# One core, four stages: weight loads on ScalarE's queue, and places of a written-out order moved

## The chip, the cores and the metric

The kernel runs on one core of one Trainium2 chip. Its time is the device time of one execution in microseconds. Before the change the median of 3 runs is 2157.19 us (2152.95 to 2161.05).

## The reference

Four layers follow each other on 2048 tokens of width 1024, in float32. Each is `x = x + layernorm(layer(layernorm(x)))`, except that the last takes x as it is.

- L0 attention: a small state-space network of depth 4 (stage A here).
- L0 feed-forward (stage B): `w2(silu(w1 x) * (w3 x))`, weights that repeat four times along their input, and low-rank parts.
- L1 attention (stage C): `q = x Wq`, `k, v = x Wkv`; 32 heads of queries of width 32 in 8 groups that share k and v; causal softmax; `ctx Wo + bo`.
- L1 feed-forward (stage D): `x W_org`, and a mixture of low-rank parts with softmax coefficients.

The kernel takes the batch of stage C as 2 of 1024 tokens: 16 "heads" of the program (2 batches, 8 groups), each of four query heads.

## The kernel before

**Precision.** Projections run as three passes of a 32-bit format with fewer bits: a value is split into a high part (a ScalarE copy) and a low part (a subtraction on VectorE or GpSimd), and TensorE sums high x high, high x low and low x high. A "part" of a weight matrix is split once, in stage B, and stored to DRAM as `pre_d`. That is done in 36 pieces: ScalarE issues the load (`act_pre_load`, L1263) and makes the high part (`act_pre_hi`, L1275), GpSimd makes the low one (`pool_pre_lo`, L1283), ScalarE issues the store in the next column (`act_pre_store`, L1279). Stage B goes through 16 tiles of 128 tokens with six columns each; every engine has its own written-out order of one column, and a piece is worked on in every second column. TensorE's `pe_fold` (L1108) in column 3 waits for ScalarE's copy `act_xt` of column 2.

**Stage C** is one order of 768 places, S = 48 o + s, for heads o = 0 to 15. At each place TensorE computes a block of scores (`pe_score`, L2086), and one of the blocks of the next heads whose row maxima are needed (`pe_amax`, L2068, 60 places ahead; VectorE takes the maximum, L2381 and L2385). ScalarE takes the exponential (L2253). Every fourth to eighth place TensorE multiplies with V (L2101). GpSimd and VectorE add up P for the softmax's sums; in the heads BY_ROUND (4, 5, 14, 15) TensorE sums half of it. Score banks and maxima banks are rings of three each.

Between them lie the projections ("jobs") of the coming heads. A job is 16 steps of three matmuls in two halves of eight; the list JOBS (L1594) gives the places of the steps and the two places where SyncE's copies of its parts stand. After a half ScalarE copies the high part (`act_job`, c_qh) and VectorE subtracts for the low part (`dve_job`, L2370, c_ql); before the subtraction it waits until the copies of the other half before it have landed. Then SyncE issues twelve DMAs of 64 KB (`sp_place`, L1874 for Q, L1863 for K) that put the parts into Q4 or K4; `pe_amax` of head o reads them first at place 48 o - 60. The weights of a job come by `sp_w` (L1820) from `pre_d` in pieces of 512 KB, and those of the output projection by `sp_wo` (L1828), two DMAs for each of 8 chunks. Both stand on SyncE's queue, at the places `next_at` (one after the last step of a job's third and fourth quarter) and WO_IN.

SyncE's queue is one order too. At each place it has, in this sequence: the steps of `sp_finish` (L1884); the row of maxima of the next head at s = 40 (`sp_mrow`, L1881, read by the first score of the next head); `sp_place`; `sp_w`; `sp_wo`. `sp_finish` turns the sums of half a head into reciprocals for all partitions: step 0 sends the sums to DRAM once ScalarE has copied them (c_cS, s = 6 or 22), step 1 reads them (L1896), VectorE takes the reciprocal, step 2 writes it (L1899), step 3 broadcasts it in four DMAs (L1903), step 4 stores the head's context (L1907). GpSimd then multiplies (`pool_mul`, L2448) in rounds 0 and 4 of the next head; a round is four places. A DMA waits in this queue for its semaphore, and all that is behind it waits too.

RELOAD gives 16 places at which ScalarE's queue brings the split x of batch 1 back, 512 KB each. At the end of stage C the first tiles of the output projection run in TensorE's order (TILES; `pe_early`, L2744); for them ScalarE makes `act_hi`, VectorE `dve_lo` (L2885, both inputs in SBUF). The last maxima (place 707) are turned by TensorE at place 710 (`pe_mrow`, L2074).

## Time and profile before

| | us |
|---|---|
| median of 3 runs | 2157.19 (2152.95 to 2161.05) |
| the profiled execution | 2154.8 |
| its span, at a mean granted clock of 0.973 | 2153.0 |
| TensorE busy | 2002.1 (93%) |
| VectorE, GpSimd, ScalarE busy | 1423.2 (66%), 1064.7 (49%), 933.4 (43%) |

A busy share is the time in which an engine has an instruction running. Times in the rows count from the start of the span. Stage B takes about 390 to 800 us, the 768 places of stage C 958 to 1700 us: about 44 us for an ordinary head.

### The profile page before, as it was taken

Reading aid. Unit: us, or ns where it says so; the run is one execution under the profiler, and the core shown is the slowest. Engines: PE = TensorE matmul, PEld = TensorE weight load, DVE = VectorE, ACT = ScalarE, POOL = GpSimd, SP = SyncE. Lnnn points to the kernel's source line nnn. Section 1 sums busy time; section 2 is a strip of 40 time slices with the busy share of each in tenths; the row PEclk is TensorE's granted clock in tenths of the full one; section 3 lists DMA queues with packets and bytes.
Section 4 is the critical chain, followed back from the end, with each engine's and each line's share of the span. In section 5 each row is a group of like instructions: output and inputs, shape, how many; then the busy total and the mean of one; then the engine's idle time right before and its main releaser. Section 6 shows DMA issues by size and latency. Waiting matters only on the chain. (4 is left out here: it accounts for less than half of the span.)

```text
span 2153.0 us, 30681 instructions
## 1 busy us (share of the span) xinstructions
PE 2002.1 (93%) x10444; PEld 1451.0 (67%) x10444; DVE 1423.2 (66%) x3201; ACT 933.4 (43%) x1938; POOL 1064.7 (49%) x914
## 2 busy tenths in 40 slices
PE   5889886999999999989999899999998999999998
PEld 4644545778788878855666466665654687888887
DVE  7877667777777763177776477677776677654433
ACT  5645685333333323115554455555555433323211
POOL 1444586666666530008886488688884343220000
PEclk9999988999999999989999999999998999999999
DMA  6400376244444338532334643433253385543432
GB/s 188 173 9 1 121 232 230 94 151 167 162 167 167 123 129 305 156 95 57 79 81 111 188 117 80 113 98 97 64 165 117 95 271 183 180 168 132 142 123 97
DMA packets 153435, 292.12 MB, mean 136 GB/s; under 512 B 28750, under 2 KB 69582, under 8 KB 153152
## 3 DMA queue, kind: packets, MB, share of 16 engines
q1 hardware_dynamic: 124224, 241.93, 35.4%
q10 hardware_dynamic: 29056, 48.24, 6.8%
q8 instruction: 83, 1.36, 0.3%
q14 instruction: 72, 0.59, 0.1%
HBM read 163.48 MB, written 94.90 MB: 120 GB/s over the span
## 5 line engine op out<-in xcount | busy, mean ns | idle before, releaser
L2253 ACT ACTIVATE c_P<-PS 128x512 f32<-128x512 f32 (+3 forms) x768 | 349.1, 496 | 342.0 <-PE PS L2086 193.2
L2068 PE MATMUL PS<-c_K,c_Q 96*128 96x512 f32 (+3 forms) x768 | 276.8, 371 | 20.2 <-DVE cst L2385 8.8
L2086 PE MATMUL PS<-c_Q,c_K 97*128 97x512 f32 (+3 forms) x768 | 275.7, 373 | 17.1 <-ACT c_P L2253 9.8
L2498 POOL TENSOR_TENSOR c_S<-c_S,c_P 128x1024 f32<-128x1024 f32 (+3 forms) x94 | 242.0, 2575 | 20.3 <-DVE c_S L2334 12.9
L2086 PEld LDWEIGHTS PS<-c_Q,c_K 97*128 97x128 f32 x768 | 147.4, 193 | 140.0 <-ACT c_P L2253 96.3
L2381 DVE TENSOR_REDUCE cst<-PS 128x1 f32<-128x512 f32 x256 | 175.8, 687 | 77.0 <-PE PS L2068 76.7
L2068 PEld LDWEIGHTS PS<-c_K,c_Q 96*128 96x128 f32 x768 | 149.9, 195 | 77.0 <-DVE cst L2385 28.8
L214 POOL TENSOR_TENSOR maskw<-maskw,mhalf 128x1 f32<-128x1 f32 x64 | 37.7, 590 | 329.9 <-DVE maskw L172 317.6
L1432 DVE SCALAR_TENSOR_TENSOR b_pr<-b_g,b_a 128x460 f32<-128x460 f32 x192 | 180.8, 977 | 1.7
L2385 DVE CUSTOM_DVE_ANT_0 PS<-PS,maskw,cst 128x128 f32<-128x128 f32 (+3 forms) x256 | 142.8, 558 | 53.2 <-PE PS L2068 34.0
L2475 POOL TENSOR_SCALAR_AFFINE_SELECT c_P<-c_P 128x512 f32<-128x512 f32 x128 | 87.4, 683 | 159.8 <-ACT c_P L2253 159.8
L2385 DVE CUSTOM_DVE_ANT_0 PS<-PS,maskw 128x128 f32<-128x128 f32 (+3 forms) x256 | 124.3, 507 | 47.9 <-PE PS L2068 46.3
L1134 PE MATMUL PS<-b_w13h,b_xsh 128*128 128x460 f32 (+1 forms) x384 | 148.0, 385 | 5.9 <-DVE b_xsl L1403 5.9
L2101 PE MATMUL PS<-c_P,c_V 128*32 128x512 f32 (+3 forms) x1536 | 152.3, 502 | 0.4 <-ACT c_P L2253 0.4
L1136 PE MATMUL PS<-b_w13h,b_xsl 128*128 128x460 f32 (+1 forms) x384 | 143.6, 374 | 0.0
L1135 PE MATMUL PS<-b_w13l,b_xsh 128*128 128x460 f32 (+1 forms) x384 | 143.5, 374 | 0.0
L1311 ACT ACTIVATE b_g<-PS 128x460 f32<-128x460 f32 x96 | 53.2, 554 | 202.2 <-PE PS L1136 88.6
L2721 PE MATMUL PS<-c_xth,d_xh 128*128 128x512 f32 x344 | 135.1, 393 | 0.0
L2722 PE MATMUL PS<-c_xtl,d_xh 128*128 128x512 f32 x344 | 134.0, 390 | 0.0
L1530 POOL TENSOR_TENSOR b_gp<-b_g 128x230 f32<-128x230 f32 x96 | 88.9, 926 | 52.6 <-DVE b_g L1417 52.6
L2042 PE MATMUL PS<-c_xth,c_w 128*128 128x512 f32 x272 | 112.3, 413 | 2.0 <-ACT c_V L2199 0.6
L2043 PE MATMUL PS<-c_xtl,c_w 128*128 128x512 f32 x272 | 108.2, 398 | 0.0
(305 smaller groups left out, 4845.5 us busy)
## 6 DMA issues: line engine op xcount, KB each, us to landing
pre_d<-b_pre ACTq DMA_DIRECT2D x36, 512.0 KB, 2.8
c_w<-pre_d SPq DMA_DIRECT2D x34, 512.0 KB, 4.0
a_xin<-in_x SPq DMA_DIRECT2D x32, 512.0 KB, 4.3
d_x<-scr SPq DMA_DIRECT2D x32, 512.0 KB, 4.8
c_Q<-c_qh SPq DMA_DIRECT2D x240, 64.0 KB, 2.0
scr<-a_xin SPq DMA_DIRECT2D x16, 512.0 KB, 5.7
b_xn<-scr SPq DMA_DIRECT2D x16, 512.0 KB, 6.7
b_x<-scr SPq DMA_DIRECT2D x16, 512.0 KB, 5.8
```

Of the source, the lines that this page charges most:

```text
L1134: e.matmul(o, self.xsh[:, par, i, :], wh[:, v, i, :], start=i == 0 and not late, stop=False, skip_group_check=True)
L1135: e.matmul(o, self.xsh[:, par, i, :], wl[:, v, i, :], start=False, stop=False, skip_group_check=True)
L1136: m = e.matmul(o, self.xsl[:, par, i, :], wh[:, v, i, :], start=False, stop=i == 1 and bool(late), skip_group_check=True)
L1432: e.scalar_tensor_tensor(out=self.prod[r][:, 0:n], in0=g, scalar=0.5, in1=self.a2[:, a:a + n], op0=MUL, op1=MUL, accum_out=self.u2[:, r, c ...
L2068: e.matmul(bank[:, 0:hi - lo], self.Q4[0:96, 4 * (o % 3) + g, 128 * t:128 * t + 128], self.K4[0:96, HEADS[o % 8], lo:hi], start=True, stop ...
L2086: e.matmul(self.k.bank(i % 3)[:, 0:hi - lo], self.K4[0:97, HEADS[o % 8], 128 * kt:128 * kt + 128], self.Q4[0:97, 4 * (o % 3) + g, lo:hi], ...
L2101: m = e.matmul(k.bank(5)[32 * g:32 * g + 32, lo - 512 * half:512], self.V[:, kt, o // 8, HEADS[o % 8], :], P[:, g, 0:hi - lo], start=kt == ...
L2253: e.activation(self.P[:, R % 3, g, 0:hi - lo], self.k.bank(i % 3)[:, 0:hi - lo], ACT.Exp, scale=SCALE).then_inc(self.exp_s.s, 1)
L2381: e.tensor_reduce(m, r, AX, ALU.max).then_inc(self.mx_s.s, 1)
L2385: e.tensor_tensor_reduce(out=r, in0=r, in1=self.maskw[:, 512 - n:512], scale=1.0, scalar=m if lo > 0 else -3.0e38, op0=ADD, op1=ALU.max, a ...
L2498: e.tensor_tensor(S[:, gs, 512 - n:512], S[:, gs, 512 - n:512], P[:, gs, 0:n], ADD).then_inc(self.psum_s.s, 1)
L2721: e.matmul(o, h, wh[:, c, cols], start=c == 0, stop=False)
```

## The change

In stage B `act_pre_hi` moves behind the other copies of its column, and `pool_pre_lo` behind `pool_gf` and `pool_x`. In stage C `sp_w` and `sp_wo` become `load_w` and `load_wo`, called in ScalarE's order at the same places after `act_job`, with the same waits. VectorE's part of a job moves one place on. In `q_job` the second half's steps move two places on, and the copies of part 1 one place (from s = 23 to s = 24, where step 0 of `sp_finish` stands ahead of them); K2, K3 and jobs 7 and 11 move by one to five places; RELOAD, WO_IN and TILES have new places; the second half's finish of head 4 comes five places later, with its multiplication in round 7; the early tiles' parts of the output projection move one to three places on. In `StageC.sp` (outside the places) only the two names change.

```
@@ -1342,8 +1342,6 @@
                 if last is not None:
                     self.act_pre_store(e, last)
                 self.act_silu(e, t, c)
-                if p is not None:
-                    self.act_pre_hi(e, p)
                 if c in (0, 2):
                     self.act_ghi(e, t - 1, c // 2)
                 if t == 1 and c < 3:
@@ -1359,6 +1357,8 @@
                         self.act_low(e, t + 1)
                 if t > 1 and c == 4:
                     T.act_x(e, t - 2)
+                if p is not None:
+                    self.act_pre_hi(e, p)
                 if now is not None:
                     self.act_pre_load(e, now)
                 if t == 1 and c == 5:
@@ -1549,12 +1549,12 @@
                     T.pool_y(e, t - 1)
                 if t + 1 < NT and c == 3:
                     self.pool_xsum(e, t + 1)
+                self.pool_gf(e, t, c)
                 p = self.pre_at(t, c, 1)
+                if t > 1 and c == 3:
+                    T.pool_x(e, t - 2)
                 if p is not None:
                     self.pool_pre_lo(e, p)
-                self.pool_gf(e, t, c)
-                if t > 1 and c == 3:
-                    T.pool_x(e, t - 2)
                 if t == 1 and c < 3:
                     self.w2lo(e, 2 * c)
         T.pool_x(e, 14)
@@ -1585,7 +1585,7 @@
 def q_job(o):
-    return o, q_slots(48 * o - 112, 2, 48 * o - 94, 2), (48 * o - 95, 48 * o - 73)
+    return o, q_slots(48 * o - 112, 2, 48 * o - 92, 2), (48 * o - 95, 48 * o - 72)
@@ -1593,19 +1593,19 @@
 JOBS = [("K0", None, None), ("K1", None, None), (0, None, None), (1, None, None), (2, None, None)]
 JOBS += [q_job(3), q_job(4), q_job(5), (6, q_slots(172, 2, 190, 2), (194, 206)),
-         ("K2", q_slots(208, 1, 219, 1), (217, 228)), (7, q_slots(231, 1, 243, 1), (242, 260)), q_job(8), q_job(9), q_job(10),
-         ("K3", q_slots(405, 1, 416, 1), (414, 425)), (11, q_slots(428, 1, 438, 2), (437, 454)), q_job(12), q_job(13),
+         ("K2", q_slots(208, 1, 220, 1), (218, 233)), (7, q_slots(235, 1, 247, 1), (245, 262)), q_job(8), q_job(9), q_job(10),
+         ("K3", q_slots(407, 1, 418, 1), (416, 427)), (11, q_slots(430, 1, 441, 2), (439, 457)), q_job(12), q_job(13),
          q_job(14), q_job(15)]
 JOB = {job[0]: n for n, job in enumerate(JOBS)}
-RELOAD = [239 + 2 * n for n in range(4)] + [255 + 2 * n for n in range(4)] + [263 + 3 * n for n in range(8)]
-WO_IN = {644 + 6 * c: c for c in range(8)}
-TILES = {711 + 4 * n: (0, n) for n in range(8)} | {745 + 4 * n: (1, n) for n in range(5)}
+RELOAD = [244 + 2 * n for n in range(4)] + [256 + 2 * n for n in range(4)] + [264 + 2 * n for n in range(8)]
+WO_IN = {644 + 8 * c: c for c in range(8)}
+TILES = {714 + 4 * n: (0, n) for n in range(8)} | {747 + 4 * n: (1, n) for n in range(5)}
 LAST = [(14, r) for r in range(7, 12)] + [(15, r) for r in range(6, 12)]
@@ -1912,7 +1912,7 @@
     def finish_at(self, S, step):
-        late = 5 if S >= 720 or 432 <= S < 480 else 0
+        late = 5 if S >= 720 or 240 <= S < 288 or 432 <= S < 480 else 0
         first, second = ((S - f[step] - d) // 48 if (S - f[step] - d) % 48 == at else -1
                          for f, at, d in zip(self.FINISH, (16, 0), (0, late)))
         return 2 * first if first >= 0 else 2 * second - 1 if second > 0 else None
@@ -1973,10 +1973,6 @@
                     self.sp_mrow(e, o + 1)
                 if S in self.place_at:
                     self.sp_place(e, *self.place_at[S])
-                if S in self.next_at:
-                    self.sp_w(e, *self.next_at[S])
-                if S in WO_IN:
-                    self.sp_wo(e, WO_IN[S])
                 if S in (692, 724, 746):
                     self.then.sp_first(e, S)
         self.sp_finish(e, 30, 4)
@@ -2298,17 +2294,21 @@
                     self.act_evac(e, 2 * o, 0)
                 if S in self.evac_at:
                     self.act_job(e, *self.evac_at[S])
+                if S in self.next_at:
+                    self.load_w(e, *self.next_at[S])
+                if S in WO_IN:
+                    self.load_wo(e, WO_IN[S])
                 if S in RELOAD:
                     self.act_reload(e, RELOAD.index(S))
                 if s == 39 and o < 15:
                     self.act_mrow(e, o + 1)
                 if S in (699, 701):
                     self.then.act_hi(e, 0, (S - 699) // 2)
-                if S in (727, 743):
-                    self.then.act_hi(e, 1, int(S > 727))
+                if S in (728, 744):
+                    self.then.act_hi(e, 1, int(S > 728))
                 if S == 758:
                     self.then.act_y(e, 0)
-                if S == 760:
+                if S == 762:
                     self.then.act_hi(e, 2, 0)
         self.act_evac(e, 31, 0)
@@ -2414,8 +2414,8 @@
                 A = S + 48 + LEAD
                 if A < 768:
                     self.dve_amax(e, A // 48, A % 48)
-                if S in self.evac_at:
-                    self.dve_job(e, *self.evac_at[S])
+                if S - 1 in self.evac_at:
+                    self.dve_job(e, *self.evac_at[S - 1])
                 if s in (27, 28) and o not in BY_ROUND:
                     self.dve_pair(e, o, s - 25)
                 if s in (35, 36) and (o, BOTH) not in LAST and o < 15:
@@ -2426,16 +2426,16 @@
                 for n in {708: [0], 712: [1], 716: [2], 720: [3], 724: [4], 747: [5], 751: [6], 757: [7], 761: [8]}.get(S, ()):
                     for g in range(4):
                         self.dve_last(e, n, g)
-                if S == 704:
+                if S == 707:
                     for half in range(2):
                         self.then.dve_lo(e, 0, half)
-                if S in (729, 744):
-                    self.then.dve_lo(e, 1, int(S > 729))
-                if S == 746:
+                if S in (730, 745):
+                    self.then.dve_lo(e, 1, int(S > 730))
+                if S == 748:
                     self.then.dve_y(e, 0)
                 if S == 755:
                     self.then.T[0].dve_y_nm(e, 0)
-                if S == 762:
+                if S == 764:
                     self.then.dve_lo(e, 2, 0)
         for n in (9, 10):
             for g in range(4):
@@ -2474,7 +2474,7 @@
                 if lo == 128 * kt:
                     e.affine_select(out=P[:, :, 0:128], in_=P[:, :, 0:128], compare_op=ALU.is_ge, fill=0.0, base=0,
                                     pattern=[[0, 4], [1, 128]], channel_multiplier=-1).then_inc(self.diag_s.s, 1)
-                if o > 0 and r in ((0, 7) if o in (9, 15) else (0, 4)):
+                if o > 0 and r in ((0, 7) if o in (5, 9, 15) else (0, 4)):
                     self.pool_mul(e, 2 * o - (2 if r == 0 else 1))
                 if (o, r) == (15, 7):
                     self.then.T[0].pool_y(e, 0)
```

## Rows read from the trace of the kernel before

**Rows 1.** Who waited for whom, TensorE, 950 to 1700 us: total us, times, longest us.

```profile
PE PS L2086 <- ACT c_P L2253: 9.8, 25, 3.8
PE PS L2086 <- DMA c_Q<-c_mT: 7.2, 3, 5.1
...
PE PS L2074 <- DVE cst L2385: 5.4, 3, 3.2
...
PE PS L2744 <- ACT c_mT L2212: 0.8, 1, 0.8
...
PE PS L2042 <- DVE c_ql L2370: 0.5, 1, 0.5
```

**Rows 2.** Windows: length; busy us by engine; granted clock; DMA share; GB/s.

```profile
1192.00:1199.00 7.00, 6.52 (x17) 5.36 (x18) 2.92 (x9) 2.39 (x4) 1.88 (x2) 0.52 0.69 195
...
1229.80:1233.20 3.40, 3.40 (x13) 2.23 (x15) 1.24 (x3) 1.96 (x5) 3.40 (x2) 0.50 0.96 250
1612.10:1618.90 6.80, 6.66 (x36) 4.55 (x36) 3.46 (x13) 3.26 (x6) 6.63 (x7) 0.50 0.68 248
1649.60:1656.40 6.80, 6.04 (x20) 3.59 (x20) 6.67 (x12) 1.57 (x6) 0.64 (x1) 0.50 0.24 82
```

**Rows 3.** Time line of SyncE's queue, 1176 to 1189 us: start, us, instruction.

```profile
1176.52 0.32 SPq L1899 DMA_DIRECT2D rec_d<-cst  x1
...
1183.05 1.22 SPq L1863 DMA_DIRECT2D c_K<-c_qh  x2
...
1186.04 1.98 SPq L1903 DMA_DIRECT2D c_cS<-rec_d  x4
1188.12 0.53 SPq L1881 DMA_DIRECT2D c_Q<-c_mT  x1
```

**Rows 4.** Time line of GpSimd in head 5; in brackets idle us before.

```profile
1225.13 1.27 POOL L2448 TENSOR_TENSOR c_cH<-c_cH,c_cS 128x512 f32<-128x512 f32 x1 [11.27 <-DMA c_cS<-rec_d]
```

**Rows 5.** Time line of TensorE at place 288; landing of L1881's 16 DMAs.

```profile
1249.16 0.50 PE L2086 MATMUL PS<-c_Q,c_K 97*128 97x512 f32 x1 [0.69 <-DMA c_Q<-c_mT]
...
DMA to landing us min/median/max: 2.1/2.2/4.3
```

**Rows 6.** Time lines of SyncE's queue and TensorE, place 672.

```profile
1607.90 0.53 SPq L1881 DMA_DIRECT2D c_Q<-c_mT  x1
...
1612.24 0.80 PE L2086 MATMUL PS<-c_Q,c_K 97*128 97x512 f32 x1 [1.37 <-DMA c_Q<-c_mT]
```

**Rows 7.** Time lines of VectorE and GpSimd, places 706 to 711.

```profile
1642.26 4.74 DVE L2885 TENSOR_TENSOR d_xl<-d_in,d_xh 128x512 fp32r<-128x512 f32 x2
...
1642.88 2.38 POOL L2467 TENSOR_TENSOR c_S<-c_S,c_P 128x1024 f32<-128x1024 f32 x1
```

**Rows 8.** Who waited for whom: TensorE in stage B; ScalarE's SiLU, whole span.

```profile
PE PS L1108 <- ACT b_xT L1254: 3.5, 4, 1.2
...
ACT b_g L1311 <- POOL b_pre L1285: 18.5, 16, 1.4
```

**Rows 9.** Time lines of TensorE and ScalarE, head 12; landing of L1874's DMAs.

```profile
1543.11 0.44 PE L2068 MATMUL PS<-c_K,c_Q 96*128 96x384 f32 x1 [0.32 <-DVE cst L2381]
...
1546.15 0.58 ACT L2261 COPY c_cS<-PS 128x512 f32<-128x512 f32 x1
...
1556.65 0.23 PE L2068 MATMUL PS<-c_K,c_Q 96*128 96x128 f32 x1
...
DMA to landing us min/median/max: 1.9/2.0/6.9
```

**Rows 10.** Time lines of VectorE and TensorE, head 9.

```profile
1412.39 0.69 DVE L2370 TENSOR_TENSOR c_ql<-PS,c_qh 128x512 fp32r<-128x512 f32 x1 [0.76 <-ACT c_qh L2206]
...
1423.52 0.30 PE L2068 MATMUL PS<-c_K,c_Q 96*128 96x128 f32 x1
```

**Rows 11.** Lines L2227 (ScalarE's queue) and L1820 (landing): ns min/median/max.

```profile
L2227 ACTq DMA_DIRECT2D c_xth<-x_d x8: 366/366/388, 1187.2 to 1242.3; - x8
...
DMA to landing us min/median/max: 3.3/4.0/8.5
```

More of the change, by code:

```diff
@@ L1344, in act @@
                 self.act_silu(e, t, c)
-                if p is not None:
-                    self.act_pre_hi(e, p)
                 if c in (0, 2):
@@ L1361, in act @@
                     T.act_x(e, t - 2)
+                if p is not None:
+                    self.act_pre_hi(e, p)
                 if now is not None:
@@ L1551, in pool @@
                     self.pool_xsum(e, t + 1)
+                self.pool_gf(e, t, c)
                 p = self.pre_at(t, c, 1)
+                if t > 1 and c == 3:
+                    T.pool_x(e, t - 2)
                 if p is not None:
                     self.pool_pre_lo(e, p)
-                self.pool_gf(e, t, c)
-                if t > 1 and c == 3:
-                    T.pool_x(e, t - 2)
                 if t == 1 and c < 3:
@@ L1586, in q_job @@
 def q_job(o):
[L1588 removed]
+    return o, q_slots(48 * o - 112, 2, 48 * o - 92, 2), (48 * o - 95, 48 * o - 72)
 JOBS = [("K0", None, None), ("K1", None, None), (0, None, None), (1, None, None), (2, None, None)]
 JOBS += [q_job(3), q_job(4), q_job(5), (6, q_slots(172, 2, 190, 2), (194, 206)),
[L1596 to L1597 removed]
+         ("K2", q_slots(208, 1, 220, 1), (218, 233)), (7, q_slots(235, 1, 247, 1), (245, 262)), q_job(8), q_job(9), q_job(10),
+         ("K3", q_slots(407, 1, 418, 1), (416, 427)), (11, q_slots(430, 1, 441, 2), (439, 457)), q_job(12), q_job(13),
          q_job(14), q_job(15)]
 JOB = {job[0]: n for n, job in enumerate(JOBS)}
[L1601 to L1608 removed]
+RELOAD = [244 + 2 * n for n in range(4)] + [256 + 2 * n for n in range(4)] + [264 + 2 * n for n in range(8)]
+WO_IN = {644 + 8 * c: c for c in range(8)}
+TILES = {714 + 4 * n: (0, n) for n in range(8)} | {747 + 4 * n: (1, n) for n in range(5)}
 LAST = [(14, r) for r in range(7, 12)] + [(15, r) for r in range(6, 12)]
@@ L1801, in sp_wv, with load_w @@
                     ).then_inc(self.wld[n].s, 16)
-    def sp_w(self, e, m, half):
+    def load_w(self, e, m, half):
         if m >= len(JOBS) - 1:
@@ L1913, in finish_at @@
     def finish_at(self, S, step):
-        late = 5 if S >= 720 or 432 <= S < 480 else 0
+        late = 5 if S >= 720 or 240 <= S < 288 or 432 <= S < 480 else 0
         first, second = ((S - f[step] - d) // 48 if (S - f[step] - d) % 48 == at else -1
@@ L1934, in sp_first @@
         elif i == 2:
-            self.sp_w(e, 0, 0)
-            self.sp_w(e, 0, 1)
+            self.load_w(e, 0, 0)
+            self.load_w(e, 0, 1)
             self.sp_x(e, 4)
@@ L1945, in sp @@
             if u == 11:
-                self.sp_w(e, 1, 0)
-                self.sp_w(e, 1, 1)
-        self.sp_w(e, 2, 0)
+                self.load_w(e, 1, 0)
+                self.load_w(e, 1, 1)
+        self.load_w(e, 2, 0)
         for n in (0, 1):
@@ L1951, in sp @@
                 self.sp_place(e, n, part)
-        self.sp_w(e, 2, 1)
+        self.load_w(e, 2, 1)
         self.sp_place(e, 2, 0)
-        self.sp_w(e, 3, 0)
-        self.sp_w(e, 3, 1)
+        self.load_w(e, 3, 0)
+        self.load_w(e, 3, 1)
         self.sp_place(e, 2, 1)
-        self.sp_w(e, 4, 0)
+        self.load_w(e, 4, 0)
         self.sp_place(e, 3, 0)
-        self.sp_w(e, 4, 1)
-        self.sp_w(e, 5, 0)
+        self.load_w(e, 4, 1)
+        self.load_w(e, 5, 0)
         self.sp_place(e, 3, 1)
@@ L2300, in act @@
                     self.act_job(e, *self.evac_at[S])
+                if S in self.next_at:
+                    self.load_w(e, *self.next_at[S])
+                if S in WO_IN:
+                    self.load_wo(e, WO_IN[S])
                 if S in RELOAD:
@@ L2306, in act @@
                     self.then.act_hi(e, 0, (S - 699) // 2)
-                if S in (727, 743):
-                    self.then.act_hi(e, 1, int(S > 727))
+                if S in (728, 744):
+                    self.then.act_hi(e, 1, int(S > 728))
                 if S == 758:
                     self.then.act_y(e, 0)
-                if S == 760:
+                if S == 762:
                     self.then.act_hi(e, 2, 0)
@@ L2428, in dve @@
                         self.dve_last(e, n, g)
-                if S == 704:
+                if S == 707:
                     for half in range(2):
                         self.then.dve_lo(e, 0, half)
-                if S in (729, 744):
-                    self.then.dve_lo(e, 1, int(S > 729))
-                if S == 746:
+                if S in (730, 745):
+                    self.then.dve_lo(e, 1, int(S > 730))
+                if S == 748:
                     self.then.dve_y(e, 0)
@@ L2437, in dve @@
                     self.then.T[0].dve_y_nm(e, 0)
-                if S == 762:
+                if S == 764:
                     self.then.dve_lo(e, 2, 0)
@@ L2476, in pool @@
                                     pattern=[[0, 4], [1, 128]], channel_multiplier=-1).then_inc(self.diag_s.s, 1)
-                if o > 0 and r in ((0, 7) if o in (9, 15) else (0, 4)):
+                if o > 0 and r in ((0, 7) if o in (5, 9, 15) else (0, 4)):
                     self.pool_mul(e, 2 * o - (2 if r == 0 else 1))
```

16 lines of the change are left out of this document (3 added, 13 removed).

## The prediction

> **What bounds the kernel now.** I read the views in this order: the page, for the busy shares; who waited for whom on TensorE, for the attention stage; the windows, for the clock after each long wait; then the time line of each engine that ends such a wait. TensorE is busy 93% of the span, so only its waits, and the clock that they cost, can be won. In the attention stage (958 to 1700 us) the waits fall into two kinds [rows 1]: many of 0.2 to 0.7 us in the ordinary heads, and a few long ones: 5.1 us for c_mT's copy (7.2 in 3), up to 3.8 us for an exponential, up to 3.2 us for the maxima that the transpose at L2074 reads. After the long ones the windows show the granted clock at 0.50 to 0.52 (1.2 GHz) for 3.4 to 6.8 us, with TensorE busy in them [rows 2]: it then does half of what it does at 2.4 GHz, so such a window costs half its length: 3.4 + 1.7 + 3.4 + 3.4 us.
>
> **What each long wait is.** (1) Before place 240, 5.12 us. SyncE's queue is the late one: rec_d at 1176.52, twelve copies of K2's second part up to 1186.0, four broadcasts, and only at 1188.12 the row of maxima [rows 3]. (2) In head 5 an exponential waits 3.8 us [rows 1], because GpSimd stood 11.27 us, until 1225.13, for the broadcast that its multiplication takes, with all sums of P behind it [rows 4]. (3) Before place 288, 0.69 us, again that row; it landed 4.3 us after its issue at worst, where 2.2 is the median [rows 5]. (4) Before place 672, 1.37 us: issued at 1607.90, landed about 1612.2 [rows 6]. (5) At place 710, 3.24 us, and 0.76 behind it for the first early tile: VectorE's two special subtractions took 4.74 us where one is 0.7, beside GpSimd's sum at 1642.88 [rows 7].
>
> **The change part by part** (gains are minus).
>
> *Low parts and copies in the feed-forward stage.* The high copy goes behind the copies of the next tile, so L1108 no longer waits: 3.5 us in 4 waits [rows 8]. Against it: GpSimd's low part now stands behind two sums (1.03 and 0.65 us), and ScalarE's store, which precedes the next SiLU, waits for it; it already did so 16 times, 18.5 us [rows 8]. In column 0 the SiLU of column 1 comes about 1.1 us later, and the product behind it has some 0.9 us before TensorE asks: 0 to 0.4 us in each of 12 tiles. Between -3.5 and +1.3 us; I take -3.0, since late loads (the usual case) already keep GpSimd at that time.
>
> *Place 240.* K2's second part goes from place 228 to 233, behind the row of maxima (232). From rec_d at about 1177 the broadcasts follow when it has landed (some 2 us) and take 2 us; the row is issued at about 1181 instead of 1188.1 and lands by 1183.5, against TensorE at 1187.4: the 5.1 us and the half clock behind them go: **-8.5**. What is late next is the second part: its twelve copies end at 1189.5 and land 2 us later, as VectorE's part of job 7 (now place 244, about 1191.8) asks for them: none to 0.5 us. K2's second half one place later takes the wait for c_ql: **-0.5** [rows 1].
>
> *Head 5.* The multiplication goes from round 4 to 7, sums of head 4 five places on. The 3.8 + 1.7 + 0.7 us go if nothing else is late. But SyncE, by my count: part 0 of job 7 until about 1200, write and read of the sums 1202.6, reciprocal 1207, broadcasts 1210 to 1212, part 1 of job 7 until 1218 to 1219.6, with TensorE at place 276 (the first use of it) at about 1222. The reloads of x1, 16 of them and now two places apart, run beside it; a copy then landed after up to 6.9 us where 2.0 is the median [rows 9]. So a wait of 0 to 3 us at 276, and as much again for the row before 288. I take 3.0 of the 6.2 back: **-3.2**, between -6.2 and +2.
>
> *Ordinary heads.* Second halves start at place 4 instead of 2 and end at 18 instead of 16. The VectorE part of a job moves one place on. What goes is part of the two waits around places 20 to 22 (the longer 0.32 [rows 9]), where TensorE had no projection beside the scores. The copies of part 1 now stand at place 24, behind the send of the sums, which waits for c_cS of place 22. In head 12 that copy began at 1546.15; its end 0.6, the send 0.6, twelve copies at 0.63 each (two took 1.22 and a gap [rows 3]), and 1.4 from the end of the last issue to landing (the median of 2.0 from its start, less 0.6) make 1556.2, and the maxima that read it start at 1556.65 [rows 9]: a margin of 0.4 us, which the faster head uses up. Net **-3.0** for ten such heads, between -5 and +5.
>
> *Head 9.* Job 11's second half ends at place 455 instead of 452; c_ql came at 1412.39, the maxima that read its copies start at 1423.52 [rows 10]. Three to four places later is 1416; with 7.5 and 1.4 us that is 1425.3: about 2 us of waiting, and half a chance of 1.7 us of clock: **+2.9**, between 0 and +5.
>
> *Loads on ScalarE's queue.* 27 pieces and 16 of Wo. No wait of theirs is open when ScalarE gets there: TensorE has done the step one place earlier. An issue there is 0.37 us and lay beside a running exponential [rows 11]. Cost 0; if it did stand in the way, 43 x 0.37 = 16 us, less what the ring of three banks absorbs; below nothing if SyncE's freed 0.4 us each lets copies out. I take 0, the nearest row.
>
> *Place 672.* Without Wo on SyncE the row goes out 0.5 us earlier, but the broadcasts before it wait for the landing of rec_d. Wo's 1 MB pieces every 8 places instead of 6 still run beside it. The copies of job 15 land later too (Wo's first pieces now run beside them), which costs at place 660 what 672 no longer does. Of 1.37 + 3.4 I take **-2.3**, between 0 and -4.8.
> The Trainium skill, "DMA: Bandwidth & Descriptors", section "Issuing engines are not separate DMA queues", says that DMAs of all issuing engines share the same engines and that a second issuer only saves issue time; the same page's "Queues, rings and completion order" says that a DMA engine alternates between queues. By the first the row still takes 4.3 us, by the second it would not stand behind Wo. The trace bears out the first: before place 288 the row was just as slow with the bulk on ScalarE's queue [rows 5].
>
> *Place 710.* The last maximum is of place 707, and the two subtractions go behind it (704 to 707): the transpose waits for nothing of theirs. Early tile (0, 0) at 714 no longer meets c_mT's copy (0.76). All 4.0 + 3.4 us go, less 0.5 for VectorE's sums, now 0.5 late for the exponential of 712: **-6.9**, between -7.4 and -3.
> The Trainium skill, "SBUF — State Buffer", section "Who interferes with whom", has a VectorE instruction with two SBUF inputs wait for the whole of a GpSimd one that reads SBUF; the 4.74 us agree. By it the subtraction, reached at about 1644.5, would still be held until 1645.3, off the path.
>
> Sum: -3.0 - 8.5 - 0.5 - 3.2 - 3.0 + 2.9 - 2.3 - 6.9 = -24.5 us. The profiled execution took 2154.8 us (span 2153.0), so 2130.3 for it; the median of the runs is 2.4 us above it, so **2132.7**, say 2133.
>
> **Rivals.** (A) *The moved places become waits.* The copies of head 5 and head 9 and the row before 672 stay as late as now; nothing is won in ordinary heads or in the feed-forward stage: -8.5 - 0.5 - 6.9 + 4 = -12, 2145. For it: landings of 4 to 7 us while loads run [rows 5, 9]; against it: SyncE is free of loads. (B) *Small copies are freed from the bulk.* The row lands in 2.2 us everywhere: 672 wins 4.8 and head 5 some 5: 2129. Against it: place 288. (C) *Slower: part 1 behind the sums.* The margin of 0.4 us is negative in the 11 heads whose part goes at place 24 or later. With loads beside it a copy lands 4 instead of 2 us after issue: 1.6 to 2 us of waiting per head, and from about 1.4 us, as at 672, the clock halves after it. 11 x (1.4 + 1.7) = 34 us against 27.4 won elsewhere: +7, 2164; it decides once copies land some 1.8 us later than the median. Against it: the loads of those heads are issued at places 11 and 19, and such a load landed 4.0 us after its issue [rows 11], before the copies end. (D) *The row of maxima doesn't hang on SyncE's order* but on VectorE's reciprocal, and the new order only shifts the wait: within 3 us of 2157.
>
> **How the numbers follow.** Forecast 0.55, A 0.22, B 0.08, C 0.08, D 0.07. What a measurement can tell from no change is about 0.5%, 10.8 us, that is 2146.4 and 2168. Faster: forecast, B and three quarters of A: 0.80; same: the rest of A and D, 0.12; slower: 0.08. The lowest sum of the bounds that I believe at once is -36 (2121); above, A reaches to 2147. Range 2120 to 2147.
>
> **What would show it.** At place 240 and at 710 no wait over 0.5 us and no half clock behind them; L1108 without waits; the row of maxima of head 5 issued before K2's second part; no GpSimd wait of 11 us in head 5. A wait of L2068 for c_Q's copies at places 276 and 468 of 1 to 3 us shows the two costs; such a wait in every ordinary head shows C. The forecast is wrong if the long waits come back at the next place, or if ScalarE's exponentials start late behind load issues.

## The result and the profile after

The changed kernel takes **2179.66 us** (median of 4 runs, 2174.78 to 2183.68) against 2155.7 us for the kernel before in the same session: ratio 1.0107 [1.0076, 1.0139]. It is 1% slower where 1% faster was forecast. The profiled execution took 2174.78 us, its span is 2173.1 us, the mean granted clock 0.977. Stage C's lines stand 4 lower than before (L2086 is now L2082, L2068 L2064, L2129 L2125, L2253 L2249); stage B's are the same.

By stages and heads of the two traces (from the first score of a head to that of the next; the last column is the changed kernel with stage B's two moves undone, e1 below):

| us | before | after | forecast | found | e1 |
|---|---|---|---|---|---|
| stage B, first to last up-projection | 451.9 | 481.7 | -3.0 | **+29.8** | 451.7 |
| heads 4 and 5 (places 192 to 287) | 116.6 | 110.6 | -12.2 | -6.0 | 109.7 |
| ten ordinary heads | 448.4 | 448.4 | -3.0 | 0.0 | 447.7 |
| head 9 | 45.8 | 53.1 | +2.9 | +7.3 | 51.9 |
| heads 13, 14, 15 | 132.5 | 122.4 | -9.2 | -10.0 | 121.8 |
| everything else | 957.8 | 956.8 | 0 | -1.0 | 959.5 |

The profiled execution is the fastest of its four, so the traces differ by 20.1 us where the medians differ by 24.

First who waited for whom on TensorE in the whole span (engine, line, what it waited for: total us, times, longest us). Before, the first of these lines was 7.9 us in 3 waits, 6.6 of them in one at the start of the stage; from 390 us on the gated value, b_g, was late once, by 0.2 us.

```profile
PE PS L1156 <- DVE b_g L1417: 29.3, 13, 4.9
...
PE PS L1134 <- DVE b_g L1417: 6.5, 11, 0.8
```

Nearly all of it lies in stage B. There TensorE stands idle 40 us instead of 15: 25 of the 30 us; the other 5 are longer busy time, for which no cause is shown. VectorE's product waits for ScalarE's SiLU, and the same view of ScalarE, from 390 to 870 us, says why that is late; its first line stood at 18.5 us in 16 waits [rows 8]:

```profile
ACT b_g L1311 <- POOL b_pre L1285: 67.4, 24, 3.3
...
ACT b_y L234 <- DMA pre_d<-b_pre: 44.9, 11, 4.3
```

The second existed before as well, once:

```profile
ACT b_y L234 <- DMA pre_d<-b_pre: 2.0, 1, 2.0
```

The time line of ScalarE in columns 4 and 5 of one tile (start, us, instruction, in brackets idle us before), kernel before:

```profile
425.59 0.61 ACT L1277 CAST b_pre<-b_raw 128x512 fp32r<-128x512 f32 x1
...
427.60 0.34 ACTq L1281 DMA_DIRECT2D pre_d<-b_pre  x1
...
432.44 0.38 ACTq L1271 DMA_DIRECT2D b_raw<-in_wq  x1
433.45 1.21 ACT L234 ACTIVATE b_y<-PS,maskw 128x1024 f32<-128x1024 f32 x1 [0.76 <-DVE maskw L180]
435.04 0.55 ACT L1311 ACTIVATE b_g<-PS 128x460 f32<-128x460 f32 x1 [0.38 <-PE PS L1156]
```

and the same column after:

```profile
426.65 1.25 ACT L239 ACTIVATE b_y<-b_x,maskw 128x1024 f32<-128x1024 f32 x1 [0.56 <-DVE maskw L207]
427.80 0.60 ACT L1277 CAST b_pre<-b_raw 128x512 fp32r<-128x512 f32 x1
430.35 0.33 ACTq L1281 DMA_DIRECT2D pre_d<-b_pre  x1
...
436.77 0.38 ACTq L1271 DMA_DIRECT2D b_raw<-in_wq  x1
437.20 1.21 ACT L234 ACTIVATE b_y<-PS,maskw 128x1024 f32<-128x1024 f32 x1 [4.27 <-DMA pre_d<-b_pre]
438.31 0.55 ACT L1311 ACTIVATE b_g<-PS 128x460 f32<-128x460 f32 x1
```

The high copy starts 2.2 us later, behind the long L239; GpSimd's low part, the next row, starts at 429.03, where it was at 426.28; so the store goes out 2.75 us later.

```profile
429.03 1.29 POOL L1285 TENSOR_TENSOR b_pre<-b_raw,b_pre 128x512 fp32r<-128x512 f32 x1
```

**And the next load, in ScalarE's own order, waits until that store has landed** (`act_pre_load` waits on `pre_out`, though what it overwrites, `raw`, is last read by the low part). Now the store lands at 436.75, 6.4 us after its issue, and ScalarE stands in front of the load, with L234 and the next SiLU behind it; the row of L234 shows 4.27 us. One late copy has become a late SiLU, product and rank matmul (L1156).

The trace before had this wait already, at its limit. The same store (427.60) took

```profile
DMA to landing us min/median/max: 4.8/4.8/4.8
```

so it landed at 432.42, and the load went out 0.02 us later: ScalarE already stood at it, for 0.3 us at most, and this lay within the 0.76 us for which L234 had to wait for VectorE anyway. Of the 35 loads of that kernel that wait for a store, 24 went out 0.02 us behind its landing; in the changed kernel all 35 do. ScalarE's view of waits does not show this, since it lists waits of computing instructions and not of DMA issues: one has to set the landing of each store beside the issue of the load behind it. Of the 4.3 us by which this load is later than before, 2.75 are the later store and 1.6 its slower landing; two transfers of 512 KB that SyncE had issued at 428.3 and 428.8 ran beside it until 434.2 and 435.5.

In the attention stage, TensorE from 978 to 1725 us, against [rows 1]:

```profile
PE PS L2064 <- DVE cst L2385: 11.4, 21, 2.9
PE PS L2125 <- POOL c_S L2498: 6.3, 11, 0.6
PE PS L2082 <- ACT c_P L2249: 4.0, 14, 0.6
...
PE PS L2064 <- DMA c_Q<-c_qh: 2.9, 1, 2.9
...
PE PS L2125 <- DVE cst L2385: 2.0, 1, 2.0
...
PE PS L2038 <- DVE c_ql L2370: 1.0, 1, 1.0
PE PS L2082 <- DMA c_Q<-c_mT: 0.9, 1, 0.9
```

The three waits for c_mT's copy (7.2 us) are one of 0.9, the exponential's 9.8 are 4.0, and the transpose's 3.2 and the early tile's 0.8 are gone: those moves did what they were to do. Other waits have come. The long ones with their places, 262 and 277 in head 5, 454 in head 9, and 661 in head 13. (From here on a wait has the number of the next score behind it. The maximum or sum that waits stands one place earlier in the order: 277, 469 and 661 are the 276, 468 and 660 of the prediction.)

```profile
1241.22 0.44 PE L2064 MATMUL PS<-c_K,c_Q 96*128 96x384 f32 x1 [2.90 <-DVE cst L2385]
...
1259.12 0.44 PE L2064 MATMUL PS<-c_K,c_Q 96*128 96x128 f32 x1 [2.58 <-issue]
...
1439.16 0.64 PE L2125 MATMUL PS<-c_S,cst 128*32 128x512 f32 x4 [2.03 <-DVE cst L2385]
...
1633.59 0.30 PE L2064 MATMUL PS<-c_K,c_Q 96*128 96x128 f32 x1 [2.92 <-DMA c_Q<-c_qh]
```

Beside each, from 0.1 us before its end to 0.9 us behind it, begins a stretch at half the clock, as those of [rows 2] (length; busy us by engine; granted clock; DMA share; GB/s):

```profile
1241.90:1248.70 6.80, 6.80 (x33) 3.73 (x24) 2.97 (x10) 3.44 (x7) 3.41 (x2) 0.50 0.60 172
1259.00:1262.40 3.40, 3.27 (x14) 1.90 (x14) 0.90 (x3) 0.49 (x1) 1.72 (x1) 0.50 0.83 297
1439.90:1443.30 3.40, 3.40 (x11) 2.39 (x8) 2.00 (x5) 2.06 (x4) 2.38 (x1) 0.50 0.25 80
1634.50:1637.90 3.40, 3.40 (x17) 0.84 (x10) 0.87 (x4) 0.98 (x2) 2.90 (x1) 0.50 0.40 119
```

The first wait is VectorE's: it stands in front of a reciprocal, with the maxima behind it.

```profile
1240.49 0.25 DVE L2390 RECIPROCAL cst<-cst 128x16 f32<-128x16 f32 x1 [2.97 <-DMA cst<-sum_d]
```

SyncE's queue shows the sums' way to that reciprocal, and the copies of job 7's second part:

```profile
1229.82 0.53 SPq L1891 DMA_DIRECT2D sum_d<-c_cS  x1
1235.36 0.34 SPq L1896 DMA_DIRECT2D cst<-sum_d  x1
1240.78 0.33 SPq L1899 DMA_DIRECT2D rec_d<-cst  x1
1243.19 1.71 SPq L1903 DMA_DIRECT2D c_cS<-rec_d  x4
1245.01 0.52 SPq L1874 DMA_DIRECT2D c_Q<-c_qh  x1
...
1251.92 0.60 SPq L1874 DMA_DIRECT2D c_Q<-c_qh  x1
1252.56 0.53 SPq L1891 DMA_DIRECT2D sum_d<-c_cS  x1
```

The write of the sums and their read (a few KB each) take 5.5 and 5.1 us beside the reloads, with the DMA engines 99% busy. In the kernel before the same write held SyncE from 1203.5 to 1209.7, and away from the reloads 1.7 us (1257.5 to 1259.2); the copies end at 1252.5, TensorE asks for them at 1256.5.

### The profile page after: what moved, and what is told of

The parts are those of the page before. It is cut to its first block, busy times and chain, and to the rows that moved or that the text cites. A ratio compares the mean times of both kernels' runs of the same rounds, so it can differ in the third digit from the quotient of the medians.

```text
span 2173.1 us, 30680 instructions
## 1 busy us (share of the span) xinstructions
PE 1998.2 (92%) x10444; PEld 1449.0 (67%) x10444; DVE 1396.3 (64%) x3201; ACT 932.3 (43%) x1938; POOL 1071.2 (49%) x914
## 3 DMA queue, kind: packets, MB, share of 16 engines
q8 instruction: 83, 1.36, 0.3%
## 4 chain that ended last, share of the span: by engine, by line
PE 52%; POOL 12%; DVE 11%; DMA 7%; issue 7%; ACT 4%; SPq 4%; ACTq 2%; POOLq 0%; DVEq 0%
PE PS L2721 5%; PE PS L2722 5%; PE PS L2725 5%; PE PS L2082 4%; POOL c_S L2498 4%; PE PS L2064 4%; PE PS L2097 3%; DMA pre_d<-b_pre 3%; SPq L1874 3%; POOL b_pre L1285 2%; PE PS L2038 2%; PE PS L663 2%; PE PS L2039 2%; PE PS L2040 2%; DVE PS L2385 2%
## 5 line engine op out<-in xcount | busy, mean ns | idle before, releaser
L2249 ACT ACTIVATE c_P<-PS 128x512 f32<-128x512 f32 (+3 forms) x768 | 348.7, 496 | 328.4 <-PE PS L2082 188.0
L2064 PE MATMUL PS<-c_K,c_Q 96*128 96x512 f32 (+3 forms) x768 | 275.5, 369 | 30.2 <-DVE cst L2385 13.4
L2082 PE MATMUL PS<-c_Q,c_K 97*128 97x512 f32 (+3 forms) x768 | 272.5, 369 | 4.8 <-ACT c_P L2249 4.0
L2498 POOL TENSOR_TENSOR c_S<-c_S,c_P 128x1024 f32<-128x1024 f32 (+3 forms) x94 | 241.9, 2574 | 22.2 <-DVE c_S L2334 13.8
L2082 PEld LDWEIGHTS PS<-c_Q,c_K 97*128 97x128 f32 x768 | 146.9, 192 | 125.5 <-ACT c_P L2249 90.4
L2064 PEld LDWEIGHTS PS<-c_K,c_Q 96*128 96x128 f32 x768 | 148.9, 194 | 85.1 <-DVE cst L2385 38.0
L1432 DVE SCALAR_TENSOR_TENSOR b_pr<-b_g,b_a 128x460 f32<-128x460 f32 x192 | 161.3, 876 | 1.7
L1417 DVE TENSOR_TENSOR b_g<-b_g,PS 128x460 f32<-128x460 f32 x96 | 60.3, 629 | 127.7 <-ACT b_g L1311 127.6
```

The costliest lines, as they stand in the source:

```text
L1432: e.scalar_tensor_tensor(out=self.prod[r][:, 0:n], in0=g, scalar=0.5, in1=self.a2[:, a:a + n], op0=MUL, op1=MUL, accum_out=self.u2[:, r, c ...
L2064: e.matmul(bank[:, 0:hi - lo], self.Q4[0:96, 4 * (o % 3) + g, 128 * t:128 * t + 128], self.K4[0:96, HEADS[o % 8], lo:hi], start=True, stop ...
L2082: e.matmul(self.k.bank(i % 3)[:, 0:hi - lo], self.K4[0:97, HEADS[o % 8], 128 * kt:128 * kt + 128], self.Q4[0:97, 4 * (o % 3) + g, lo:hi], ...
L2249: e.activation(self.P[:, R % 3, g, 0:hi - lo], self.k.bank(i % 3)[:, 0:hi - lo], ACT.Exp, scale=SCALE).then_inc(self.exp_s.s, 1)
L2498: e.tensor_tensor(S[:, gs, 512 - n:512], S[:, gs, 512 - n:512], P[:, gs, 0:n], ADD).then_inc(self.psum_s.s, 1)
```

## The experiments

Each kernel was timed in turns with the kernel before on the same chip; the ratio is to that. Where two kernels' ratios lie within 0.5% of each other, I call it no difference in the time, though a trace can still place it; each trace is of one execution, and stage B or the 768 places differ by up to 5 us between kernels that are equal there.

**e1: stage B as before.** The changed kernel with both moves of stage B undone:

```
                 self.act_silu(e, t, c)
+                if p is not None:
+                    self.act_pre_hi(e, p)
...
                     T.act_x(e, t - 2)
-                if p is not None:
-                    self.act_pre_hi(e, p)
...
+                p = self.pre_at(t, c, 1)
+                if p is not None:
+                    self.pool_pre_lo(e, p)
                 self.pool_gf(e, t, c)
-                p = self.pre_at(t, c, 1)
                 if t > 1 and c == 3:
                     T.pool_x(e, t - 2)
-                if p is not None:
-                    self.pool_pre_lo(e, p)
```

> The changed kernel with both moves in stage B (the high copy late in its column, the low part behind GpSimd's sums) undone. Theory 1 (the loss is in stage B alone: 451.9 -> 481.7 us between the first and last up-projection, while stage C won 8.7): stage B takes 452 again, 1.008 less stage C's gain: 2150 us, ratio to before 0.996. Rival (stage C's gain in the trace of the changed kernel exists only because stage B's waits left its start calmer): 2156 or more, ratio 1.00.

2144.75 us, ratio 0.9947 [0.9933, 0.9961]. Stage B is 451.7 us again, and the 768 places take 731.0 us against 743.2. So the slower time is stage B's alone; the rest of the change is worth about 11 us in the time (8.7 to 12.2 by the 768 places of the two traces), half of the forecast 21.5.

**e2 and e3: the two moves of stage B, one at a time**, each put into the kernel before. e2, and below it e3:

```
                 self.act_silu(e, t, c)
-                if p is not None:
-                    self.act_pre_hi(e, p)
...
                     T.act_x(e, t - 2)
+                if p is not None:
+                    self.act_pre_hi(e, p)
```

```
-                p = self.pre_at(t, c, 1)
-                if p is not None:
-                    self.pool_pre_lo(e, p)
                 self.pool_gf(e, t, c)
+                p = self.pre_at(t, c, 1)
                 if t > 1 and c == 3:
                     T.pool_x(e, t - 2)
+                if p is not None:
+                    self.pool_pre_lo(e, p)
```

> The kernel before with only ScalarE's high copy moved late in its column. Theory L (a loop: in column 4 the copy waits behind the 1.25 us normalisation of an older tile, so the store goes out 2.2 us later, and in column 5 ScalarE stands at the next load until that store has landed, with the normalisation and the next SiLU behind it; slack today 1 us): about +1.2 us and more in each of 12 tiles, less 3.5 us for L1108: 2166 to 2172. Rival G (the cost is GpSimd's order, the low part behind two sums, met by the SiLU of columns 1 and 3): nothing lost here, 3.5 us won, 2152.

> The kernel before with only GpSimd's low part moved behind its sums. Theory L: the store of column 4 goes out 1.8 us later and lands 0.8 us after the slack ends: +10 us, 2166. Rival G: nearly the whole loss of stage B, 2180 to 2185.

e2: 2172.69 us, 1.0076 [1.0063, 1.0089], stage B 465.7. e3: 2197.31 us, 1.0189 [1.0176, 1.0202], stage B 488.7. Each makes the store late by itself and has the wait for its landing, the same view of ScalarE in e2:

```profile
ACT b_y L234 <- DMA pre_d<-b_pre: 36.0, 11, 3.6
```

and in e3:

```profile
ACT b_y L234 <- DMA pre_d<-b_pre: 41.6, 11, 3.9
```

The moves do not add (13.8 and 36.8 us alone, 29.8 together), and e3 took far more than the 2166 us that I expected, more even than its rival's 2180 to 2185. In e3 TensorE waits at L1108 as well, 14.7 us in 11 waits, longest 1.5: the load comes late, ScalarE's high copy still stands ahead of the copy that L1108 reads, and waits for it. Only the first move takes this path away, as the forecast had it for the kernel before; these waits are 14.7 of the 31 us by which e3 lies above its expectation, and the rest stays open.

**e5: the load no longer behind the store.** The whole changed kernel; the load waits for the low part, the last reader of its buffer `raw`, and the high copy, the first writer of `pre`, waits for the store:

```
 def act_pre_load(self, e, p):
     if p > 0:
-        e.wait_ge(*self.pre_out(p))
+        e.wait_ge(*self.pre_lo(p))
...
 def act_pre_hi(self, e, p):
     e.wait_ge(*self.pre_in(p + 1))
+    if p > 0:
+        e.wait_ge(*self.pre_out(p))
```

> The whole changed kernel, with one wait of stage B at another place: the load of the next piece waits for the low part of the piece before (which ends the reading of b_raw), and no longer for its store to land; the high copy waits for that instead (it overwrites b_pre). Theory L (ScalarE stands at the load until the store has landed, 4.3 us in column 5 in the trace of the changed kernel, and the next load lands late for the copies of column 0 and 2): most of the 30 us come back, stage B 452 to 460 us instead of 481.7, 2150 to 2160. Rival G (only GpSimd's order counts: the low part behind its sums, met by the SiLU of columns 1 and 3): at most 5 us, 2175 or more.

2145.53 us, 0.9954 [0.9937, 0.9971]; stage B 451.2 instead of 481.7 us, with both moves still in. ScalarE in the same column (lines behind the edit two higher):

```profile
428.03 0.60 ACT L1279 CAST b_pre<-b_raw 128x512 fp32r<-128x512 f32 x1
430.58 0.33 ACTq L1283 DMA_DIRECT2D pre_d<-b_pre  x1
...
432.59 0.38 ACTq L1271 DMA_DIRECT2D b_raw<-in_wq  x1
433.89 1.21 ACT L234 ACTIVATE b_y<-PS,maskw 128x1024 f32<-128x1024 f32 x1 [0.77 <-DVE maskw L180]
435.49 0.55 ACT L1313 ACTIVATE b_g<-PS 128x460 f32<-128x460 f32 x1 [0.38 <-PE PS L1156]
```

Copy and store are as late as in the changed kernel (430.58), the load goes out at 432.59 and nothing stands. The wait of ScalarE for GpSimd's low part has even grown in e5, and costs nothing:

```profile
ACT b_g L1313 <- POOL b_pre L1287: 80.4, 24, 4.4
```

So the load's wait for the landing accounts for the 30 us, and the wait that I had priced was nearly harmless. The rival, GpSimd's order alone, had at most 5 of them come back.

**e11: the same edit in the kernel before** (the diff of e5).

> The kernel before with only the wait for the store moved from the load to the high copy. Theory L (that wait is the loop of stage B): the load lands 3 us earlier, so the high copy no longer holds up the copies behind it; L1108's 3.5 us go: stage B 448.5, 2153. Rival (the load then lands earlier but the high copy waits for the store instead): no difference, 2156.

2155.26 us, 0.9988 [0.9978, 0.9998]; in the trace stage B is 447.9 us (451.9) and L1108's waits are gone, which is what the moves of stage B were forecast to give; the whole time does not tell it from no change. Beside it e5, with the same free load and both moves, is 3.3 us longer in this stage (451.2), within the spread of such traces: with the load free the moves show no gain over the old order.

**e7: the loads back on SyncE's queue**, the rest as e1 (below: in `sp`; the same four lines go from `act`).

```
+                if S in self.next_at:
+                    self.sp_w(e, *self.next_at[S])
+                if S in WO_IN:
+                    self.sp_wo(e, WO_IN[S])
```

> The first kernel again (stage B as before, stage C as changed), but all weight loads back on SyncE's queue at the same places. Theory 4 (the move of the loads to ScalarE's queue is worth nothing by itself; the places are): 2143 to 2147 as the first kernel. Rival (it is what makes the new places possible: 12 copies, four broadcasts and the row of maxima are each held up by a load's wait for TensorE): 5 us and more above it, 2150 or more, with the row of head 5 or 6 late again.

2144.58 us, 0.9944 [0.9928, 0.9959]: equal to e1 (0.9947). Which queue issues the loads makes no difference in the time. It only shifts a wait; TensorE around places 661 and 672 in e7

```profile
1598.45 0.30 PE L2068 MATMUL PS<-c_K,c_Q 96*128 96x128 f32 x1 [0.57 <-DMA c_Q<-c_qh]
...
1610.73 0.80 PE L2086 MATMUL PS<-c_Q,c_K 97*128 97x512 f32 x1 [1.95 <-DMA c_Q<-c_mT]
```

and in e1:

```profile
1602.74 0.30 PE L2064 MATMUL PS<-c_K,c_Q 96*128 96x128 f32 x1 [3.20 <-DMA c_Q<-c_qh]
```

In e1 TensorE has no wait at place 672, having lost more time at 661 already.

**e4: head 9 as before**, the rest as e1:

```
-("K3", q_slots(407, 1, 418, 1), (416, 427)), (11, q_slots(430, 1, 441, 2), (439, 457))
+("K3", q_slots(405, 1, 416, 1), (414, 425)), (11, q_slots(428, 1, 438, 2), (437, 454))
```

> Stage B as before, stage C as changed, but K3 and job 11 at their places of before. Theory 2 (head 9 costs 7.3 us since job 11's part 1 is copied three places later and is read by the maxima at place 468, with 3.4 us of half clock behind an earlier wait of 2.0 us): 7 us less than the first kernel of this call, 2143. Rival (the wait only moves on to the next row of maxima, since GpSimd's sums or SyncE's finish steps are late by themselves): within 2 us of it.

2146.25 us, 0.9948 [0.9935, 0.9961]: no gain over e1. Head 9 is 46.5 us instead of 51.9, but head 8 is 56.1 instead of 51.5, with waits for c_ql of 1.06 and 1.26 us and a half-clock window of 3.4. Head 9's price is not in the moves of K3 and job 11 taken alone.

**e6: K2's second part alone behind the row of maxima**, in the kernel before:

```
-("K2", q_slots(208, 1, 219, 1), (217, 228))
+("K2", q_slots(208, 1, 219, 1), (217, 233))
```

> The kernel before with one number changed: the copies of K2's second part at place 233 instead of 228 in SyncE's order, behind the row of maxima. Theory 3 (that order alone made the 5.1 us at place 240 and the half clock behind it): -8.5 us, 2147.5, and job 7's low part waits less than 1 us for the copies. Rival (the load pieces on SyncE's queue, still there, hold the row up all the same): 2156.

2158.61 us, 1.0012 [1.0000, 1.0023]. The wait before place 240 goes and comes back before place 244, longer than it was:

```profile
1197.27 0.80 PE L2068 MATMUL PS<-c_K,c_Q 96*128 96x512 f32 x1 [6.07 <-DVE cst L2385]
```

VectorE's low part of the next job waits 5.79 us for those copies, with the maxima behind it. Head 4 is 54.6 us (59.9), head 5 62.0 (56.7). So the order in SyncE's queue made the wait at 240, as forecast, but the gain needs job 7's steps moved too, as the change does.

**e8: the early tile's low parts alone at place 707**, in the kernel before:

```
-                if S == 704:
+                if S == 707:
```

> The kernel before with only VectorE's two low parts of the first early tile at place 707 instead of 704, so behind the last maximum. Theory 5: the 3.2 us at place 710 and the half clock behind it go, less 0.5: -6 us, 2150, with 0.8 us left before the early tile at 711. Rival (the exponentials behind them then wait for VectorE's sums instead): under 2 us won.

2153.2 us, 0.9985 [0.9972, 0.9999]: in the trace the 3.2 us before place 710 and the half clock behind them are gone, head 14 is 42.6 us instead of 48.2, and 0.86 us are left for the early tile, whose place this run did not move. The whole time hardly shows it: this run also waited 2.2 us at 672 and 1.6 at 288.

**e9: the reloads spread out**, the rest as e1:

```
-RELOAD = [244 + 2 * n for n in range(4)] + [256 + 2 * n for n in range(4)] + [264 + 2 * n for n in range(8)]
+RELOAD = [244 + 18 * n // 7 for n in range(8)] + [264 + 3 * n for n in range(8)]
```

> The first kernel (stage B as before, stage C as changed) with the 16 reloads of x1 spread over places 244 to 285 instead of 244 to 278. Theory 6 (head 5 won nothing because the denser reloads hold SyncE's small copies: 12 copies landing up to 7 us after issue make 3.9 us at place 277, the read of the sums 2.7 us at place 262, and 3.4 us of half clock behind them): head 5 falls from 56.9 to 53 to 54 us, 2142. Rival (SyncE's order is late by itself): within 1 us of 2145.

2143.12 us, 0.9946 [0.9931, 0.9961]. The wait at 277 is gone and head 5 is 54.4 us (56.9), but at 262 TensorE waits 3.95 us: that the reloads' spacing made that wait is not borne out. Not told from e1 in the time.

**e10: the copies of part 1 before the send of the sums**, the rest as e1 (in `q_job`):

```
-(48 * o - 95, 48 * o - 72)
+(48 * o - 95, 48 * o - 73)
```

> The first kernel with the copies of part 1 of the ordinary jobs at s = 23 again, ahead of the send of the sums. Theory 7 (rival C of the prediction, in one head alone: in head 13 the copies land beside Wo's loads and TensorE waits 3.2 us at place 661, with 1.7 us of clock; in the other heads the margin holds): head 13 falls by 2 to 4 us but the row of maxima is then late at 672, as before; net 2143 to 2145, the other heads unchanged. Rival (the position behind the sums costs in all heads): 0.5 us in each of ten heads more, 2139.

2151.98 us, 0.9969 [0.9958, 0.9979]: by the ratios 5 us slower than e1, which the time alone does not tell, and not the 2143 to 2145 us expected. In the trace the 768 places take 741.0 us, against 731.0 in e1. The wait at 661 goes, and the row of maxima is late instead, with half clock behind it; heads 5, 13 and 14 take 58.3, 47.8 and 39.3 us (56.9, 45.3 and 37.9 in e1):

```profile
1623.53 0.80 PE L2082 MATMUL PS<-c_Q,c_K 97*128 97x512 f32 x1 [3.76 <-DMA c_Q<-c_mT]
```

Rival C's mechanism, the copies behind the sums, so was real at place 661 only, and the old order is no better.

**e12: three edits together** on e1: the diffs of e5 and e10, and

```
-(11, q_slots(430, 1, 441, 2), (439, 457))
+(11, q_slots(429, 1, 440, 2), (438, 455))
```

> Stage C as changed with the copies of part 1 ahead of the sums and job 11 one place earlier (steps 429 and 440, copies 438 and 455), stage B with the orders of before and the wait for the store at the high copy. If the parts add up: -3 in stage B, -1 in ordinary heads, -3 in head 9 against the first kernel: 2138. If the waits of head 9 only move: 2142.

2147.06 us, 0.995 [0.9938, 0.9962]: no better than e1, and neither of the two expected times. Stage B gives its 3 us (448.5), and what takes them back in the time isn't shown: the 768 places take 2 us more than in e1, within their spread.

**e13 and e14: e1 with the diff of e5; and with that of e9 besides.**

> Stage C's part of the change whole (copies of part 1 at s = 24 as in the change), the orders of stage B as before, and the load of a piece waiting only for the low part before it, with ScalarE's high copy waiting for the store instead. Theory (the feed-forward stage's gain of e11 and the attention stage's gain of e1 stand beside each other; what e12 lost was lost by its copies at s = 23, as in e10): stage B 448, the 768 places 731, 2141 us, ratio 0.993. Rival (an earlier stage B brings no more than the places give back, or e12's loss was the new job 11): 2145 to 2147, 0.995, as e1 and e12.

> As e13, and the sixteen reloads of x1 spread out as in e9 (places 244 to 262, 264 to 285). Theory (spread reloads shorten head 5 by some 2 us, as e9's row showed, though the wait at place 262 stays): 2139.5, ratio 0.992, head 5 54.5 us. Rival (what head 5 wins comes back in other heads, as in e9): the same as e13 within 1 us.

e13: 2146.36 us against 2160.61, 0.9935 [0.9919, 0.995], stage B 449.1 us, the places 734.3. e14: 2142.97 us, **0.9922 [0.9906, 0.9937]**, stage B 447.8, the places 734.9. e14 has the lowest ratio of all and beats both kernels (the changed one stands at 1.0107); its interval overlaps those of e1 and e13, so that it beats these is not shown. In both traces the 768 places take 3 to 4 us more than in e1, so that stage B's gain adds to e1's is not shown either.

## Why the prediction was wrong

**The step that failed** is the first: "between -3.5 and +1.3 us; I take -3.0, since late loads (the usual case) already keep GpSimd at that time." Measured: +29.8. I asked who waits for the SiLU and for the low part, and took both bounds from these. I did not follow the copy further: low part, store, landing, and the next load, which stands in ScalarE's order and waits for the landing. e5 takes that one wait off the load and gets 30 of 30 us back. The step also used the wrong cover: the row that ScalarE "already did so 16 times" [rows 8] says that the chain high copy, low part, store had no slack on the way in, not that its end had any. The bound of +1.3 was thus no bound: of a chain that is closed by a DMA, the landing belongs to its cost. The trace before had it, for all stores of this line (L1281), and 24 loads right behind a landing:

```profile
DMA to landing us min/median/max: 2.6/2.8/5.9
```

**Place 240: right.** Row of maxima before the copies, no wait at 240, no half clock there. The 5.1 us of the wait end head 4 and the 3.4 us of clock began head 5, so head 4 was to lose 5.1 + 0.5 and lost 6.7. e6 shows that the term belonged to K2 and job 7 together.

**Head 5: mechanism right, size wrong**, the second largest miss. The 11 us of GpSimd and the 3.8 of the exponential went; so came the wait at 277, forecast as "0 to 3 us at 276" and measured at 2.58, with 1.7 us of clock that I had not added. Not foreseen was the wait at 262: the reciprocal's, 2.90 and 3.4 of clock, since the sums take 5 us each way beside the reloads, 10.7 from the write to the reciprocal where I had counted about 7 (1200 to 1207). Head 5 as a whole was to become 3.4 (clock behind 240) and 3.2 us shorter and became 0.7 longer: the term of -3.2 came out at about +4.

**Ordinary heads: 0 instead of -3.0.** The waits near places 20 to 22 shrank; a new one of 0.6 us stands at s = 6 of most of these heads, where TensorE's sum waits for GpSimd (the line L2125 <- POOL above). That TensorE gets there earlier because the second half's steps now start at s = 4 fits; it was not tried by itself. Rival C was not so in these heads, and its sum was short: 27.4 us won elsewhere has these heads' 3.0 in it and leaves out head 9's +2.9, so its own terms give 34 - 21.5, 2170 us.

**Head 9: +7.3 instead of +2.9.** The forecast wait for job 11's copies is there, 1.17 us at 469. The larger part is 2.03 us at 454, again VectorE in front of a reciprocal (idle 3.89 us before it), with a half-clock window, and 0.96 at 442 for c_ql. e4 shows that with the old places head 9 wins 5.4 us and head 8 loses 4.6.

**Loads on ScalarE at 0: right** (e7). **Places 672 and 710: right in sum**, -9.2 forecast and -10.0 found for heads 13 to 15, but by other parts: 710 gave all, head 15 two more, and the wait of 672 was not won but moved to 661 (2.92 us and its half clock). The forecast had this trade (what 660 costs, 672 no longer does) as a part of its -2.3; the two together come to about nothing. e7 against e1 shows it too. The Trainium skill's rule of the section "Issuing engines are not separate DMA queues" ("DMA: Bandwidth & Descriptors"), which the prediction weighed, is borne out: with the loads on SyncE's queue TensorE waits 1.95 us for the row (e7), with them on ScalarE's 3.20 us for the copies (e1).

**The chances.** Slower had 0.08, all of it on rival C, which asked 1.6 to 2 us in each of 11 heads. No rival had stage B in it, because its bounds were believed. With stage B left out, the change gives about 11 us (e1): rival A's sum, and half of the forecast's. The signs that the forecast named for itself were all there (240, 710, L1108, the row's issue, GpSimd, waits at 276 and 468), and one against it, long waits at other places (262, 661); none of them asked for the store's landing.

## What to carry to other kernels

When an instruction moves later in an engine's order, follow what it makes until something waits for a DMA's landing, and look on which engine's order that wait stands: there everything behind it waits too. Make such a wait as late and as narrow as the buffers allow (here on the first writer, not on the load): that alone took the ratio from 1.0107 to 0.9954, some 33 us. A wait in front of a DMA's issue on a computing engine is not in its view of waits: look for issues that follow a landing at once. A long wait that has several causes near the same limit can move on when one is taken away (240 to 244 in e6, 661 and 672 in e1 and e7, head 9 to head 8 in e4); 710, which had one cause, went with one edit (e8).

## What the runs showed of the hardware

- A store of 512 KB that lands after 2.7 us at the median took 6.4 us beside others of 512 KB (4.8 in the kernel before, issued 2.75 us earlier in its column), and small DMAs (the sums of a half head) 5.1 and 5.5 us while 512 KB pieces came in on ScalarE's queue; a 64 KB copy then landed after up to 7.1 us, where 2.0 is the median. The Trainium skill, "DMA: Bandwidth & Descriptors", section "Latency and other measured facts", puts the memory's access at 2 us under high load; here the whole of a small DMA to or from DRAM took more than twice that.
- Of TensorE's waits in the attention stage, all that were 2 us or longer had 3.4 to 6.8 us at half clock beside or behind them in the kernel after, and none of 1.36 us or less had; in the kernel before one of 1.37 us [rows 6] had, as [rows 2] show. The length of the wait alone doesn't decide it: in e2 one of 1.16 us at place 672 had 6.8 us, in e5 one of 2.06 us in head 5 (at 1230.90) none, and head 0 has 10.2 us at half clock in both kernels (from 960.1 and 989.4) with no wait over 0.7 us in the 9 us before.
- VectorE's two subtractions, 4.74 us beside GpSimd's sum [rows 7], took 1.29 us at their new place:

```profile
1675.24 1.29 DVE L2885 TENSOR_TENSOR d_xl<-d_in,d_xh 128x512 fp32r<-128x512 f32 x2
```
